# Laying the input out twice on the host and writing every loop out in a four-layer attention and mixer kernel

## The reference

```python
# layers 0 and 2: attention over the 256 tokens of an image, with a residual
q, k, v = x @ Wq + bq, x @ Wk + bk, x @ Wv + bv        # q and k have 16 channels
x = gamma * softmax(q @ k.T) @ v + x
# layer 1: a mixer in frequency space, with a residual
xh = dht2d(x)                                          # over channels and over the width
x = dht2d(soft_threshold(two_block_layers(xh, flipped(xh)))) / (W * C) + x
# layer 3: group norm (32 groups), attention with 128 channels, an output product, a residual
n = group_norm(x) * gn_gamma + gn_beta
x = (softmax((n @ wq + bq) @ (n @ wk + bk).T / sqrt(C)) @ (n @ wv + bv)) @ wo + bo + x
```

## Time and profile before

| | |
|---|---|
| time, median of 3 runs (lowest to highest) | 136.01 us (135.72 to 136.84) |
| span of the profiled execution, first to last instruction | 133.5 us |
| what lies around the span (136.01 - 133.5) | 2.5 us |
| PE busy | 118.8 us, 89% |
| ACT, DVE, POOL busy | 77.1 us, 74.4 us, 27.2 us |
| HBM read, written | 2.27 MB, 1.05 MB |
| instruction queues (q8, q14) | 5 and 7 packets, 0.08 and 0.05 MB |

### The profile page before, as it was taken

The page is one execution under the profiler, slowest core; times in us unless marked ns, Lnnn a source line. Parts: engine busy times, 40 slices in busy tenths (PEclk is TensorE's granted clock), DMA queues, the critical chain, the costliest instruction groups (busy, mean ns, idle before and its releaser), DMA issues.

```text
span 133.5 us, 2896 instructions
## 1 busy us (share of the span) xinstructions
PE 118.8 (89%) x846; PEld 109.8 (82%) x846; DVE 74.4 (56%) x323; ACT 77.1 (58%) x218; POOL 27.2 (20%) x56
## 2 busy tenths in 40 slices
PE   6908999999999999999999999999999999998300
PEld 5707899999998989998899999989999999986200
DVE  0020455555547436544374555699999999866100
ACT  4001277777774688867766777666667666775100
POOL 1000041149210311321111212061223311100000
PEclk9985699999999999999999999999999999999975
DMA  4815500000000000000000000000000011111110
GB/s 109 224 40 152 155 0 0 5 0 0 0 2 0 0 2 5 0 0 0 0 0 0 5 0 0 2 0 2 5 0 0 13 34 36 39 39 43 46 43 30
DMA packets 5016, 3.45 MB, mean 26 GB/s; under 512 B 381, under 2 KB 4605, under 8 KB 5005
## 3 DMA queue, kind: packets, MB, share of 16 engines
q1 hardware_dynamic: 3642, 2.20, 5.8%
q10 hardware_dynamic: 1362, 1.12, 3.0%
HBM read 2.27 MB, written 1.05 MB: 25 GB/s over the span
## 4 chain that ended last, share of the span: by engine, by line
PE 82%; DMA 6%; ACT 2%; SPq 1%; DVE 1%; issue 1%; DVEq 0%
PE banks L579 16%; PE banks L607 16%; PE banks L559 9%; PE banks L570 9%; PE banks L591 8%; DMA images<-in_x 6%; PE banks L549 5%; PE banks L663 3%; PE banks L655 3%; PE banks L654 3%; PE banks L624 2%; PE banks L672 2%; PE banks L638 1%; PE banks L680 1%; PE banks L640 1%; SPq L388 1%
## 5 line engine op out<-in xcount | busy, mean ns | idle before, releaser
L771 ACT ACTIVATE probs<-negated,lowest 128x256 f32<-128x256 f32 x48 | 24.2, 504 | 22.5 <-DVE negated L907 22.5
L466 POOL TENSOR_TENSOR staged<-images,one 128x256 f32<-128x256 f32 x30 | 18.3, 614 | 65.0 <-PE banks L549 29.1
L907 DVE TENSOR_SCALAR_CACHE_REDUCE negated<-banks,v 128x256 f32<-128x256 f32 x48 | 22.7, 476 | 9.7 <-PE banks L579 9.6
L607 PEld LDWEIGHTS banks<-v,probs_t 128*128 128x128 f32 x192 | 25.0, 191 | 2.1 <-ACT probs_t L779 0.9
L607 PE MATMUL banks<-v,probs_t 128*128 128x128 f32 x192 | 25.5, 276 | 0.7 <-ACT probs_t L779 0.7
L579 PE MATMUL banks<-xt,u 128*128 128x256 f32 x96 | 25.5, 388 | 0.0
L895 DVE TENSOR_TENSOR v<-banks,vb 128x258 f32<-128x258 f32 x24 | 10.2, 424 | 17.1 <-PE banks L570 17.1
L579 PEld LDWEIGHTS banks<-xt,u 128*128 128x128 f32 x96 | 16.8, 195 | 1.6 <-ACT u L763 0.2
L924 DVE SCALAR_TENSOR_TENSOR images<-banks,inverse,images 128x128 f32 (+1 forms) x48 | 14.6, 344 | 4.9 <-PE banks L607 4.3
L559 PE MATMUL banks<-xt,uw 128*128 128x256 f32 x48 | 15.6, 407 | 0.0
L570 PE MATMUL banks<-vw,xt 128*128 128x129 f32 x96 | 15.2, 282 | 0.3 <-DVE y L935 0.3
(11 more groups left out here) (99 smaller groups left out, 170.2 us busy)
## 6 DMA issues: line engine op xcount, KB each, us to landing
constants<-in_constants SPq DMA_DIRECT2D x1, 450.0 KB, 5.0
out<-images SPq DMA_DIRECT2D x7, 64.0 KB
images<-in_x ACTq DMA_DIRECT2D x2, 192.0 KB, 5.9
out<-images SPq DMA_DIRECT2D x8, 48.0 KB
values<-in_values ACTq DMA_DIRECT2D x1, 320.0 KB, 2.9
images<-in_x SPq DMA_DIRECT2D x2, 144.0 KB, 4.0
layer<-in_layer ACTq DMA_DIRECT2D x1, 256.5 KB, 4.7
images<-in_x SPq DMA_DIRECT2D x4, 48.0 KB, 3.3
```

Of the source, the lines that this page charges most:

```text
L466: pool.tensor_tensor(flat(staged[:, half]), flat(images[:, i]), one[:, :].to_broadcast([TILE, TILES * C]), ALU.mult).then_inc(image_staged ...
L607: mm = nc.tensor.matmul(mixed_bank(half)[:, tile * C:(tile + 1) * C], probs_t[:, half, m, tile * TILE:(tile + 1) * TILE], v[:, half, m, 0: ...
L771: nc.scalar.activation(probs[:, half, tile, :], negated[:, half, tile, :], ACT.Exp, bias=lowest[:, half, tile:tile + 1], scale=-1.0, accum ...
L907: nc.vector.tensor_scalar(negated[:, half, tile, :], energy_bank(half)[:, tile * TOKENS:(tile + 1) * TOKENS], v[:, half, tile, C:CV], FMAX ...
```

## The change

- The host hands over x in two layouts: `x_rows` (tokens on partitions, in the tiles' order) and `x_t` (channels on partitions). `x_t` is loaded into a new buffer `xt_in`, and layer 0 takes U, V and E from it: T and `move_xt` go from layer 0. `x_rows` goes to `images`, for the residual alone in layer 0.
- The result is written in the tiles' layout, one DMA for an image, and the host puts it in order.
- `staged`, `stage` and the wait for it go. T in layers 2 and 3 and the mixer's first product read `images`, after a wait for the layer before (`layer_done`).
- All loops are written out.
- `values` is split: `values0` (layer 0's) comes first. Six warm-up matmuls become three. The mixer's matrices are built at the start of POOL's program.

```diff
-WARM_UP = 6
+WARM_UP = 3
-LOADS = [(0, 1), (1, 2), (2, BATCH)]
+XT_LOADS = [(0, 1), (1, 2), (2, 4), (4, BATCH)]
+X_LOADS = [(0, 2), (2, BATCH)]
...
-def in_order(engine, slot):
...
-        with engine.Fori(head // 2, (BATCH - tail) // 2) as pair:
...
+def in_order(slot):
+
+    for at in range(LAYERS * BATCH + 2):
+        slot(Job(min(at // BATCH, LAYERS - 1), at - min(at // BATCH, LAYERS - 1) * BATCH, at % 2))
...
+        def channels_first(job):
+
+            return xt_in[:, job.image] if job.layer == 0 else xt[:, job.half]
...
+        def load_xt(engine, k):
+            begin, end = XT_LOADS[k]
+            engine.dma_start(xt_in[:, begin:end].rearrange("p b t k -> p (b t k)"),
+                             x_t_d[:, begin * TOKENS:end * TOKENS]).then_inc(xt_loaded[k], 16)
+
+        def load_x(engine, k):
+            begin, end = X_LOADS[k]
+            at = TILES * C
+            engine.dma_start(images[:, begin:end].rearrange("p b t c -> p (b t c)"),
+                             x_rows_d[:, begin * at:end * at]).then_inc(x_loaded[k], 16)
+
+        def store(engine, i, tile, tiles):
+            engine.dma_start(out[:, i, tile:tile + tiles, :],
+                             images[:, i, tile:tile + tiles, :]).then_inc(stored, 16)
 
         @block.sync
         def _(sp):
             sp.dma_start(small[:, :], small_d).then_inc(small_loaded, 16)
-            load(sp, 0, range(TILES))
-            load(sp, 1, range(TILES))
-            load(sp, 2, (0,))
+            load_xt(sp, 0)
+            load_xt(sp, 1)
+            load_xt(sp, 2)
+            load_xt(sp, 3)
             sp.dma_start(blocks[:, :, :, :], blocks_d).then_inc(blocks_loaded, 16)
             sp.dma_start(constants[:, :], constants_d).then_inc(constants_loaded, 16)
...
-            pool.wait_ge(x_loaded[2], 2 * DMAS * 16)
-            for n in range(LAYERS):
...
+            mixer_matrices()
+            for i in range(BATCH):
                 inverse_deviation(i, i % 2)
...
             def transpose_x(job):
 
                 n, i, half = job
...
+                pe.wait_ge(layer_done[n - 1], (i + 1) * TILES)
...
                 for tile in range(TILES):
                     mm = nc.tensor.transpose(xt_bank(half)[:, tile * TILE:(tile + 1) * TILE],
-                                             source[:, tile, :], ident)
+                                             images[:, i, tile, :], ident)
...
-                elif attends(this) and not norms(this):
+                elif attends(this) and not norms(this) and this.layer > 0:
                     transpose_x(this)
...
+            act.dma_start(values0[:, :], values0_d).then_inc(values0_loaded, 16)
+            load_x(act, 0)
             act.dma_start(values[:, :], values_d).then_inc(values_loaded, 16)
             act.dma_start(layer3[:, :], layer3_d).then_inc(layer3_loaded, 16)
-            load(act, 2, (1,))
+            load_x(act, 1)
...
+                if n == 0 and i in (X_LOADS[0][0], X_LOADS[1][0]):
+                    dve.wait_ge(x_loaded[0 if i == 0 else 1], 16)
```

More of the change, by code:

```diff
@@ L52 @@
 FMAX = 3.0e38
[L55 to L58, removed]
-LOADS = [(0, 1), (1, 2), (2, BATCH)]
+ROWS = [[0, 8, 1, 2, 3, 13, 14, 15], [4, 5, 6, 7, 9, 10, 11, 12]]
+XT_LOADS = [(0, 1), (1, 2), (2, 4), (4, BATCH)]
+X_LOADS = [(0, 2), (2, BATCH)]
 FIXED = 4
@@ L126, in job_at @@
 def job_at(slot, back):
[L129 to L135, removed]
+    at = slot.layer * BATCH + slot.image - back
+    if not 0 <= at < LAYERS * BATCH:
+        return None
+    return Job(at // BATCH, at % BATCH, at % 2)
 def attends(job):
@@ L150, in is_job @@
 def is_job(job, layer, image):
-    return isinstance(job.image, int) and job[:2] == (layer, image)
-def in_order(engine, slot):
[L159 to L163, removed]
-        with engine.Fori(head // 2, (BATCH - tail) // 2) as pair:
[L165 to L170, removed]
+    return job[:2] == (layer, image)
+def in_order(slot):
+    for at in range(LAYERS * BATCH + 2):
+        slot(Job(min(at // BATCH, LAYERS - 1), at - min(at // BATCH, LAYERS - 1) * BATCH, at % 2))
 SMALL_AT = {0: 0, 2: 3 * C + 1}
@@ L224, in build @@
         act_warm = sb("act_warm", [C, 1])
[L225 removed]
         images = sb("images", [TILE, BATCH, TILES, C])
[L232 removed]
+        xt_in = sb("xt_in", [C, BATCH, TILES, TILE])
         xt = sb("xt", [C, 2, TILES, TILE])
@@ L300, in build @@
         layer3_loaded = sem("layer3_loaded")
-        x_loaded = [sem(f"x_loaded{k}") for k in range(len(LOADS))]
+        xt_loaded = [sem(f"xt_loaded{k}") for k in range(len(XT_LOADS))]
+        x_loaded = [sem(f"x_loaded{k}") for k in range(len(X_LOADS))]
         stored = sem("stored")
@@ L624, in forward_tokens @@
                     mm = nc.tensor.matmul(sums_and_differences[:, :, at:at + pairs],
-                                          staged[:, half, tile, :],
+                                          images[:, i, tile, :],
                                           halves(views["forward"][:, 2 * at:2 * (at + pairs)]),
@@ L700, in slot @@
                     plain_products(2)
-                if mixes(back3):
+                if mixes(back3) and not is_job(now, MIXER + 1, 2):
                     backward_channels(back3)
@@ L741, in _ @@
             plain_products(0)
-            in_order(pe, slot)
+            in_order(slot)
         @block.scalar
@@ L822, in slot @@
                     normalize(this)
-                elif attends(this):
+                elif attends(this) and this.layer > 0:
                     move_xt(this)
```

157 lines of the change are left out of this document (55 added, 102 removed).

## The result

The changed kernel takes 124.91 us in the median (123.19 to 126.63, four runs), the kernel before 135.97 (135.72 to 136.84) beside it. The ratio is 0.905, with an interval of 0.901 to 0.910: 9.5% faster, by the two shorter runs. The prediction was 123.1 us, with a range of 120.8 to 126.0.

A forecast was written before the change was run, and what follows sets the result against it. It took PE to bound the middle, with layer 0's loop through `move_u` close behind, and slow starts and stores the ends: 133.5 - 7.1 - 0.35 - 0.8 - 4.6 = 120.65, with 2.5 added 123.1 us; range 120.8 to 126.0.

The forecast's parts named there:

- the likeliest case: Whole kernel: the forecast of 123.1 us holds, with its own range 121.5 to 124.8; chance 0.70.
- the start: Up to E of image 1: halved warm-up and earlier image loads bring it from 18.74 to 11.6, 7.1 us less.
- the stores: End of kernel: one DMA of 128 rows for each image replaces three, 4.6 us less, between 2.2 and 4.6.
- the time around the span: Whole kernel: 2.5 us added to the summed span, since the median 136.01 lies above the span of 133.5.
- full-clock start: Start of kernel: with full clock from 5.5 on, U at 6.0 and E of image 1 at 10.6, 1.0 us earlier.
- the full T: Layer 0, rival: PE's T was the whole bound, slots fall by 0.22 to 3.07, total 122.3 us; chance 0.08.
- T in layer 0: Layer 0, five slots: T leaves PE, but a 3.22 us loop through `move_u` limits the gain to 0.35, not 1.1.
- copies on POOL: Layer 3: without POOL's copies `mean_sum` falls from 446 to about 160 ns and slots to 3.69, 0.8 us less.
- loops: Whole kernel: writing the loops out gives 0, since a branch back costs nothing that shows.
- that sign: Start of kernel: forecast wrong if U comes early but the slots of images 0 and 1 exceed 3.5 us.
- The transfers stay narrow: Stores, rival: 128 rows of 1 KB also move at 43 GB/s, the end gives nothing, 127.7 us; chance 0.05.
- Fetches: Whole kernel, rival: written-out program cannot be fetched fast enough, ends slower than before, seven exposed stalls give 139; chance 0.04.

The follow-up runs named there:

- `again`: The changed kernel run once more with no edit: 123.39 us, ratio 0.905 against the kernel before; its profile is of a shorter run, time 123.03, span 121.2.
- experiment 7: Experiment 2's kernel with T's two transposes put back on PE in layer 0, into a bank nobody reads: 122.94 us, ratio 0.890 to the kernel before.
- the first profile: The changed kernel, unedited, profiled in one of its longer runs: span 124.6 us.
- Experiment 2: The changed kernel with loads reordered: ACT issues `values` and `layer3` before its x, SP holds back the last x_t piece: 123.10 us, ratio 0.904.
- experiment 8: Experiment 2's kernel with U and `move_u` of each image done one slot earlier in layer 0: 122.39 us, ratio 0.897 to the kernel before.
- the padded one: The changed kernel with each store a pair of 64-row halves, one padding row between them in the output: 127.42 us, ratio 0.934.
- the adjoining one: The changed kernel with each store's plain rows described as a pair of adjoining 64-row halves: 124.55 us, ratio 0.911.
- experiment 4: The kernel before with only x and the output in tile layout, moved as plain 128-row transfers: 124.45 us, ratio 0.913.
- experiment 5: The kernel before with only its loops written out: 135.13 us, ratio 0.990.
- experiment 9: The changed kernel with twelve warm-up instructions in place of six: 123.39 us, ratio 0.906 to the kernel before.
- experiment 11: The changed kernel with reordered loads, U one slot ahead in layer 0, and twelve warm-up instructions: 121.43 us, ratio 0.891 to the kernel before.

## Why the prediction was right, and where its steps were not

The total was right, and the likeliest case was the one that held, in five of the changed kernel's eight runs. That it was met so closely (123.1 against 123.03) is luck: the start and T gave 1.1 and 0.35 less than I took, the stores, the copies with the loops, and the time around the span 0.7, 0.2 and 0.7 more. And the 124.91 is a median between two pairs of runs, of which the longer lies above my range (126.47 and 126.63 against 126.0). The range itself does not follow from its terms: a full-clock start and the full T give 123.1 - 1.0 - 0.75 = 121.35, and not 120.8. Term by term, against `again`:

| term | predicted | measured |
|---|---|---|
| start | -7.1 | -6.0 |
| T in layer 0 | -0.35 | -0.1, given back in the next slot |
| copies on POOL | -0.8 | -1.02 in the slots: 0.42 copies, 0.24 loops, 0.36 the double copy |
| loops | 0 | in the line above |
| stores | -4.6 | -5.3 |
| span | 120.65 | 121.2 |
| around the span | 2.5 | 123.03 - 121.2 = 1.8 |

**Start.** U was at 6.69 (6.5 forecast) and E of image 0 at 8.56 (8.3). The step that failed is the loop from there to image 1: I took 3.22 + 0.1 and got 12.75 - 8.56 = 4.19. The earlier trace rows had 3.92 for this step already. What it consists of: 3.07, PE's own work in a later slot without T; 0.54, since E of image 0 at half clock holds U back for 1.41 us (8.56 to 9.97) and not 0.87; 0.32 of waiting for `layer3`; and 0.25, since this slot has the products of layer 3 (11.14 to 12.28, 1.14 us) where a later one has M. The sum is 4.18. The 0.87 (12.75 to 13.62) and M's 0.89 (14.05 to 14.94) are in the rows of `again` above.

With full clock and no wait the step still is 3.57, T's 0.22 in it (7.53 to 11.10, experiment 7). I had written that I am wrong if U comes early and the slots of images 0 and 1 are longer than 3.5: the first is, 4.19 here and 7.55 in the first profile, so for the start that sign came true. "With full clock, all of it comes 1.0 earlier" was right for U (5.76 in the first profile), and wrong for the rest, since I gave the weights 1.1 us of cover at half clock and didn't carry it into the early case. There the cover was gone: `layer3` landed 8.9 us after its issue, near 11.5 and not 8.9, and PE stood 2.49 us. The rate was right: by the slices, (89 + 191) x 3.1 us and 313 x 2.7 us are 1.7 MB by 8.9, where I had 1.8. But by 11.5 it is 2.7 MB: what passed before `layer3` was a megabyte more than I put ahead of it. Experiment 2, which issues `layer3` ahead of x on ACT and holds some of x back on SP, brings its landing from 8.5 to 7.1 us after the issue.

**T in layer 0.** The mechanism was right: PE waits 0.16 for `u`, and T's removal gives no more than the loop lets through. Its length was misread, and that is the step that failed. I measured from E's start (116.92) to the next load of weights (120.14), but those are two different marks. In that very slot E's own weights begin at 116.85:

```profile
116.85 0.73 PEld L579 LDWEIGHTS banks<-xt,u 128*128 128x128 f32 x4
```

With the weights loaded in time E starts about 0.1 behind their load; when they come late, E and its weights start together (22.53 and 22.52). Measured from like to like (116.85 to 120.14) the loop is 3.29, just PE's own 3.29, so two bounds stood at the same value, and lowering one of them gives nothing. Experiment 7 shows it from one side and experiment 8 from the other. "Full T" did not happen.

**POOL and the loops.** 0.8 against 1.02, and the mechanism (`mean_sum` 446 to 160 ns) as read for the 0.42; the 0.24 are the loops, and the 0.36 are argued, not shown. That the loops cost nothing was wrong by 0.24 in layer 3 and by 0.8 in the backlog of stores, which the plain stores make moot. The fetch that the Trainium skill ("Runtime: NRT & Kernel Launch", Instruction fetch mechanics) ties to a taken branch out of the window does not show in layer 0, where the step is 3.29 with and without branches back; where the small costs elsewhere come from was not traced.

**Stores.** The landing was 1.7 and not 2.3 us, the nearest row being a load of 69 KB. The rule of the Trainium skill ("DMA: Bandwidth & Descriptors", Why a DMA increments its semaphore by 16) was put to the test by the two pairs: the padded one agrees with it, 0.14 of sixteen engines; the adjoining one, 0.44, went like plain rows, so that what counts is the pattern as it is issued. "The transfers stay narrow" is excluded.

**Fetches.** The instruction queues moved 0.14 MB in 11 packets, against 0.13 in 12 before. PE's own rows show no gap without a releaser. Its loads of weights show a few, of 0.28 to 0.67 us, in both kernels; the one ahead of the first small products grew from 0.33 to 0.65 us, and of the others none is new.

**Around the span.** 1.8 us in `again`, and also in experiment 4 and in the kernel before where a profile and its own run are compared (135.24 - 133.4). My 2.5 came from setting one profile against a median of other runs. It is 0.7 us in the direction that hid the start's miss.

## What to carry to other kernels

Before you cut work from a full engine, follow the loop that leaves it and returns, from like event to like event: if that loop is as long as the engine's own work, the cut gives nothing until the loop is shortened too. A DMA whose pattern began with a pair kept 0.14 of sixteen engines busy here, and laying the data out on the host so that 128 plain rows go at once can be worth more than all else in a change (here, in experiment 4, 11.1 of the 12.3 us of span). When a start becomes faster, check each load again against the fastest case: here a wait there cost its 2.49 us and the clock behind it.

## What was unexpected of the hardware

- **A wait and the clock after it.** In the first profile PE stood for 2.49 us in the middle of its start, and the granted clock was 0.50 from 12 to 17 us although PE was busy all the time. The kernel lost 3.3 us by it against the other runs.
- **The recorded clock and the durations don't agree at the start.** In `again` the granted clock is told as 1.00 from 3 to 9 us, while U takes 1.22 us there and 0.70 at full clock in the first profile. Durations of like instructions are the better clock.

```profile
3.00:9.00 6.00, 6.00 (x22) 5.08 (x21) 0.94 (x6) 0.47 (x1) 0.53 (x2) 1.00 0.94 242
```

- **The spread goes with the warm-up.** With six warm-up instructions the runs of a kernel differ by 1.2 to 4.3 us (eight kernels, four to eight runs each), with twelve by 0.3 to 0.7 in experiments 4, 5, 9 and 11. The kernel before, also with twelve but with PE standing 3.64 us behind them, differs by 2.0 over eleven runs; experiment 5, which stands like it, by 0.4 over four. The warm-up alone differs between `again` and experiment 9 (3.3 and 0.3) and between experiments 8 and 11 (1.2 and 0.7).
- **The price of an issue follows the pattern.** A plain store takes SP 332 ns to issue, one with a pair 514 for the same bytes:

```profile
L331 SPq DMA_DIRECT2D out<-images x8: 332/332/348, 96.6 to 118.8; - x8
```

```profile
L331 SPq DMA_DIRECT2D out<-images x8: 501/514/662, 96.8 to 118.9; - x8
```
